# Four edits to the second stage's order of work: landmarks read from PSUM, a later bias product, another split of a norm, an earlier sum

## The chip, the cores and the metric

The kernel runs on one core of a Trainium2 chip, as one launch. Its time is the device time of that core in microseconds (us), the median of the runs shown. A core has five engines that run side by side: TensorE (PE, matrix products into PSUM), VectorE (DVE), ScalarE (ACT), GpSimd (POOL) and SyncE (SP, which here issues most transfers). They wait for each other only through semaphores.

## What is computed

Sixteen samples of 128 channels by 32 by 32 pixels pass through three layers. Only the third layer's first half and its gate matter here:

```python
# second stage, attention with landmarks (8 heads, 16 landmarks, N = 1024 tokens)
q_lm, k_lm = q[:, :, lm_idx], k[:, :, lm_idx]
kernel_1 = softmax(q @ k_lm.T * scale)      # keys' landmarks against all queries
kernel_2 = softmax(q_lm @ k_lm.T * scale)
kernel_3 = softmax(q_lm @ k.T * scale)
z = kernel_2.T / fro**2                     # then six Newton steps:
for _ in range(6):
    z = 2.0 * z - z @ kernel_2 @ z
out = kernel_1 @ (z @ (kernel_3 @ v))       # then the projection, and the sum with the input
# second stage, mixture of 8 experts, the best 2 for each token
gate = softmax(xt @ Wg); topv, topi = top_k(gate, 2); topv /= sum(topv) + 1e-6
h = gelu(xt @ W1[e] + b1[e]); ye = h @ W2[e] + b2[e]; out += ye * scores[:, e]
```

Before it stand an attention layer and a convolution layer, after it a dense attention with a mixture of 16 experts. The change leaves these as they are.

## The kernel before

The program runs in three stages: attention and convolution to about 2360 us, the landmark and GELU stage (`landmark_and_gelu_phase`, from L1058) to about 3900 us, and the dense stage. The change touches the middle one.

In it, every sample passes three jobs. `front` is the landmark attention. `choice` is the gate: a norm over each token, scores, the two best experts, the routing table, and the part of the result that comes from the experts' second bias. `experts` is the work of the 23 tiles of 128 routed rows. While `experts(i)` runs, `front(i + 2)` and `choice(i + 1)` run beside it; `front(0)` and `front(1)` with `choice(0)` run ahead of all expert work.

The order is written out by hand in slots. Each engine has a generator for each job; `yield 19` means that what follows belongs behind slot 19. `side_by_side` (L1186) goes through the 46 slots of a sample, two for each tile of rows; in each slot it issues the engine's own expert step and then, job by job in the order given (`front`, `choice`, `combine`), what has fallen due. So the slots fix the order on each engine, and semaphores hold one engine back for another. A late step holds up all that is behind it on its engine.

The parts that the change and the prediction name:

- Landmarks. TensorE forms queries and keys at slots 15 and 16 (L1679, L1681), both through L1662. ScalarE moves them from PSUM to `qt` and `kt` with their biases (L1576, L1579). VectorE picks every 64th column of both, spreads it over the heads with a block mask and writes `q_lm` and `k_lm` (L1354, slot 17). TensorE then forms the first score product (L1685, slot 18) and, from `kt`, the third (L1688, slot 19).
- Newton. TensorE multiplies (L1707), VectorE copies the product out of PSUM (L1406), TensorE multiplies twice (L1710, L1711), VectorE updates both forms of z (L1409, L1410). After the first update VectorE also sums the first softmax's weights (L1414) and inverts the sum (L1416); after the second it multiplies the weights by it (L1419).
- Norm of the gate's tokens, `token_norm_steps` (L976): statistics, variance, then an inverse root of ten small operations (L58 to L65), then the scaling (L991). In `choice`, statistics and variance are issued at slot 0 and the rest at slot 4 (L1500 to L1502). Also at slot 4, and ahead of it, `front` issues L1344 and L1346, on whose result TensorE's transposes (L1672, slot 6) wait. TensorE turns the scaled tokens with L1746 at slot 8.
- Bias product. TensorE multiplies scores by the second bias in two halves (L1776, slots 34 and 36), both into the PSUM tile `pc`; VectorE adds each half to the attention's result (L1526, slots 36 and 38). The second product waits for the first addition.
- Routing. VectorE writes the row numbers (L1473, slot 30), upon which POOL scatters the tokens with 16 indirect transfers (L1321). When all have landed, SP loads the next sample's first rows (L1246), which TensorE turns at slot 45 (L1784) and ScalarE moves out of PSUM (L1631). Behind that load SP issues the next weights of the experts (L1256).
- Expert tiles: TensorE L1801 (up), ScalarE L1617 (GELU), TensorE L1811 (down).

Of the kernel before, what the change touches and what calls it, by code (L numbers as in the profile page):

```python
# [21 lines left out]
AX = mybir.AxisListType  # L22
# [3 lines left out]
N = HW * HW  # L26
NT = N // 128
HALVES = N // 512
HEADS = 8
# [1028 lines left out]
def landmark_and_gelu_phase(nc, ctx, B, io, const, maps, gn2, x1_dram, x_dram, y_dram, score_dram, out):  # L1058
# [7 lines left out]
    with ExitStack() as st:  # L1066
# [6 lines left out]
        LM = 16  # L1073
        STEP = N // LM
# [28 lines left out]
        q_lm, k_lm = small[:, 7, :], small[:, 8, :]  # L1103
# [226 lines left out]
        def _(dve):  # L1330
            b16 = const["block16"].rearrange("p (h l) -> p h l", h=HEADS)

            def front(i):
# [17 lines left out]

                for src, dst, up in ((qt, q_lm, 1), (kt, k_lm, 2)):
                    dve.wait_ge(S["qk_up"], i * 2 + up)
                    last = dve.tensor_tensor(dst[:, :].rearrange("p (h l) -> p h l", h=HEADS), b16,  # L1354
                                             src[:, 0:N:STEP].unsqueeze(1).broadcast_to((128, HEADS, LM)), ALU.mult)
                last.then_inc(S["lm_up"], 1)
                yield 19
# [41 lines left out]

                dve.tensor_scalar(zt[:, :], m2[:, :], fro[:, :], None, ALU.mult).then_inc(S["z0_up"], 1)  # L1400

                for it in range(NEWTON):
# [9 lines left out]
                    if it == 0:  # L1412
                        dve.wait_ge(S["k1_exp"], i + 1)
                        dve.tensor_reduce(sum1[:, :], k1v, axis=AX.X, op=ALU.add)  # L1414
                        dve.drain()
                        dve.reciprocal(sum1[:, :], sum1[:, :])  # L1416
                        dve.drain()
# [77 lines left out]
            def choice(i):  # L1495
# [4 lines left out]
                for n, last in enumerate(token_norm_steps(dve, xln2, tok, stats2, mv2, var2, inv2, tmp2)):  # L1500
                    if n == 2:
                        yield 4  # L1502
# [20 lines left out]
                for k in range(HALVES):  # L1523
                    yield 36 + 2 * k
                    dve.wait_ge(S["b2_ps"], i * HALVES + k + 1)
# [40 lines left out]
        def _(act):  # L1566
            def front(i):
# [9 lines left out]
                yield 16  # L1577
                act.wait_ge(S["qk_ps"], i * 2 + 2)
                act.activation(kt[:, :], pa[:, :], ACT.Identity, bias=kb[:, :]).then_inc(S["qk_up"], 1)  # L1579
                yield 21  # L1580
# [76 lines left out]
        def _(pe):  # L1657
# [7 lines left out]
            def front(i):  # L1665
# [20 lines left out]
                last.then_inc(S["s1_ps"], 1)  # L1686
                yield 19
                wide(pa, q_lm[:, :], kt).then_inc(S["s3_ps"], 1)  # L1688
                yield 21
# [48 lines left out]
            def choice(i):  # L1738
# [29 lines left out]
                for k in range(HALVES):  # L1768
                    yield 34 + 2 * k
                    if k:  # L1770
# [546 lines left out]
```

## Time and profile before

| | |
|---|---|
| time, median of 3 runs | 5388.46 us (5380.94 to 5393.68) |
| the profiled execution | 5387.68 us, span 5385.9 us |
| busy: PE, DVE, ACT, POOL | 89%, 66%, 55%, 19% of the span |
| mean granted TensorE clock | 0.96 of full speed |
| middle stage, 2360 to 3900 us | PE 1343, DVE 911, ACT 826, POOL 499 us busy |

An engine's busy share is the time in which it works on instructions. In the rows further down, a number in brackets at the end is the time for which the engine stood idle before the instruction, and what it was released by. The time of the profiled execution holds 1.8 us beside its span.

### The profile page before, as it was taken

What the parts mean: (1) busy time and instruction counts of PE and PEld (TensorE: products, weight loads), DVE (VectorE), ACT (ScalarE), POOL (GpSimd) and SP (SyncE); (2) the same over time, 40 slices, a digit from 0 to 9 for tenths busy, and PEclk for the clock granted to TensorE, in tenths of its full rate; (3) what the DMA queues carried; (4) which work ended last, traced back from release to release, by engine and by line L of the source; (5) the groups of instructions that cost most, each with busy time, mean ns of one, the idle gap of its engine ahead of it and who ended that gap; (6) DMA issues with size and microseconds to landing.
All of it is one profiled execution on the core that took longest, in us unless ns stands there. A gap on an engine that the chain in (4) does not pass through costs nothing. (4 is left out here: it accounts for less than half of the span.)

```text
span 5385.9 us, 81280 instructions
## 1 busy us (share of the span) xinstructions
PE 4780.0 (89%) x25601; PEld 2597.7 (48%) x25601; DVE 3550.8 (66%) x7443; ACT 2946.7 (55%) x5390; POOL 1020.9 (19%) x1348
## 2 busy tenths in 40 slices
PE   5888888888888886977899999898999999999999
PEld 1222222222222221325888888888855555555554
DVE  6677777777777772555566666665577677776775
ACT  2665666666665654422555555555755555455552
POOL 2211211122121212211333343433210000000000
PEclk6999999999999998977999999999999999999999
DMA  2522222222222221232455555545321111111112
GB/s 83 152 72 72 72 95 72 72 72 72 72 76 81 72 76 32 29 71 76 146 171 147 170 160 160 173 139 151 115 60 50 49 56 46 53 50 49 56 46 77
DMA packets 406292, 477.05 MB, mean 89 GB/s; under 512 B 87640, under 2 KB 249648, under 8 KB 403760
## 3 DMA queue, kind: packets, MB, share of 16 engines
q1 hardware_dynamic: 372128, 424.84, 26.0%
q0 software_dynamic: 20576, 35.55, 2.4%
q10 hardware_dynamic: 13168, 11.48, 0.8%
q8 instruction: 213, 3.49, 0.3%
q14 instruction: 207, 1.70, 0.1%
HBM read 308.54 MB, written 145.57 MB: 84 GB/s over the span
## 5 line engine op out<-in xcount | busy, mean ns | idle before, releaser
L605 ACT ACTIVATE a_probs<-ps_b 128x512 f32<-128x512 f32 x2048 | 1111.1, 594 | 786.7 <-PE ps_b L701 773.9
L461 DVE TENSOR_REDUCE a_negmax<-ps_a 128x1 f32<-128x1024 f32 x1024 | 1206.2, 1220 | 382.1 <-PE ps_a L645 373.8
L645 PE MATMUL ps_a<-a_k_stack,a_q_stack 96*128 96x512 bf16 x2048 | 629.8, 393 | 177.2 <-DVE a_negmax L461 90.2
L701 PE MATMUL ps_b<-a_q_stack,a_k_stack 99*128 99x512 bf16 x2048 | 669.8, 389 | 65.8 <-ACT a_probs L605 30.9
L1617 ACT ACTIVATE n_hidden<-n_ps_h,n_b 128x128 f32<-128x128 f32 x1472 | 420.5, 373 | 413.3 <-PE n_ps_h L1801 409.8
L714 PE MATMUL ps_o<-a_probs,a_v_ones 128*32 128x512 f32 x4096 | 560.8, 620 | 0.2 <-ACT a_probs L605 0.2
L645 PEld LDWEIGHTS ps_a<-a_k_stack,a_q_stack 96*128 96x128 bf16 x2048 | 146.0, 98 | 726.9 <-DVE a_negmax L461 470.5
L1811 PE MATMUL n_ps_xy<-n_down_weights,n_hidden 128*128 x2944 | 405.3, 281 | 55.9 <-ACT n_hidden L1617 28.9
L701 PEld LDWEIGHTS ps_b<-a_q_stack,a_k_stack 99*128 99x128 bf16 x2048 | 195.1, 99 | 484.2 <-ACT a_probs L605 247.2
L1811 PEld LDWEIGHTS n_ps_xy<-n_down_weights,n_hidden 128*128 128x128 f32 x2944 | 366.0, 194 | 86.8 <-issue 83.0
L1801 PE MATMUL n_ps_h<-n_xy,n_up_weights 128*128 128x128 f32 x2944 | 402.9, 281 | 4.2 <-DMA n_up_weights<-in_L_ffn_W_dram 2.6
L2100 ACT ACTIVATE n_down_weights<-n_ps_h 128x512 f32<-128x512 f32 x288 | 172.5, 599 | 416.9 <-PE n_ps_h L2215 313.2
L1321 POOL DMA_INDIRECT rows_scratch<-n_xln,n_index_out x256 | 257.6, 1006 | 718.5 <-DVE n_index_out L1473 641.5
L1801 PEld LDWEIGHTS n_ps_h<-n_xy,n_up_weights 128*128 128x128 f32 x2944 | 372.8, 197 | 27.3 <-issue 23.8
L1313 POOL DMA_INDIRECT n_rows<-outs_scratch,n_index_back x256 | 261.7, 1022 | 363.8 <-DMA outs_scratch<-n_xy 246.9
L417 POOL CAST a_shift<-a_shift 16x128 bf16<-16x128 f32 x192 | 54.2, 283 | 1300.7 <-DVEq L470 1283.4
L2163 PEld LDWEIGHTS n_ps_f<-n_xln,n_u_probs_t 128*128 128x128 f32 x2048 | 246.2, 192 | 67.4 <-DVE n_u_probs_t L1982 36.4
L2163 PE MATMUL n_ps_f<-n_xln,n_u_probs_t 128*128 128x128 f32 x2048 | 250.9, 276 | 8.2 <-ACT n_u_probs_t L2066 8.2
L2156 PE MATMUL n_ps_f<-n_qt 128*128 128x512 f32 x512 | 240.9, 593 | 0.0
L2069 ACT ACTIVATE n_yt_probs<-n_ps_f,e_negmax 128x1024 f32<-128x1024 f32 x128 | 142.6, 1114 | 128.6 <-DVE e_negmax L1985 128.3
L1985 DVE TENSOR_REDUCE e_negmax<-n_ps_f 128x1 f32<-128x1024 f32 x128 | 156.5, 1222 | 77.0 <-PE n_ps_f L2156 76.3
L2203 PE MATMUL n_ps_c<-n_down_weights,n_xt 128*128 128x512 f32 x384 | 198.1, 599 | 2.6 <-DVE n_down_weights L2041 2.6
(345 smaller groups left out, 7398.5 us busy)
## 6 DMA issues: line engine op xcount, KB each, us to landing
n_up_weights<-in_L_ffn_W_dram SPq DMA_DIRECT2D x368, 256.0 KB
n_up_weights<-score_scratch SPq DMA_DIRECT2D x512, 128.0 KB, 2.9
split_scratch<-a_pieces SPq DMA_DIRECT2D x180, 256.0 KB
a_q_stack<-split_scratch SPq DMA_DIRECT2D x128, 192.0 KB, 3.4
a_k_stack<-split_scratch SPq DMA_DIRECT2D x128, 192.0 KB, 4.0
rows_scratch<-n_zero SPq DMA_DIRECT2D x16, 1472.0 KB
outs_scratch<-n_xy SPq DMA_DIRECT2D x176, 128.0 KB
n_xg<-rows_scratch SPq DMA_DIRECT2D x80, 256.0 KB, 3.8
```

What stands on the lines that cost most here:

```text
L461: dve.tensor_reduce(negmax[:, b, t:t + 1], bank, axis=AX.X, op=ALU.max, negate=True).then_inc(ring_read, 1)
L605: act.activation(probs[:, m % PROBS, 512 * k:512 * k + 512], ps_b[:, k, :], ACT.Exp).then_inc(b_exp, 1)
L645: last = pe.matmul(bank[:, cols], q_stack[0:KS, h, 128 * t:128 * t + 128], k_stack[0:KS, h, cols], start=True, stop=True)
L701: pe.matmul(ps_b[:, k, :], k_stack[:, h, 128 * t:128 * t + 128], q_stack[:, h, 512 * k:512 * k + 512], start=True, stop=True).then_inc(b_u ...
L714: last = pe.matmul(ps_o[32 * j:32 * j + 32, 512 * k:512 * k + 512], v_ones[:, t, J * g + j, :], probs[:, (J * quad + j) % PROBS, 512 * k:5 ...
L1313: gp.indirect_dma_start(rows[:, k, t, :], None, y_dram[i][:, :], bass.IndirectOffsetOnAxis(index_back[:, k, t:t + 1], 0)).then_inc(gathere ...
L1321: gp.indirect_dma_start(x_dram[i][:, :], bass.IndirectOffsetOnAxis(index_out[:, k, t:t + 1], 0), xln2[:, t, :], None).then_inc(scattered, 16)
L1617: last = act.activation(hidden[:, j % 2, f, :], ps_h[j % 2][:, 128 * f:128 * f + 128], ACT.Gelu, bias=b1[:, bass.ds(e, 1), f:f + 1].rearra ...
L1801: last = pe.matmul(ps_h[j % 2][:, 128 * f:128 * f + 128], up_weights[:, j % RING, 128 * f:128 * f + 128], rows_t, start=True, stop=True)
L1811: last = pe.matmul(ps_xy[:, col:col + 128], hidden[:, j % 2, f, :], own_down[:, f, :], start=(f == 0), stop=(f == FT - 1))
L2156: last = pe.matmul(pa[:, 512 * k:512 * k + 512], qt[:, 128 * t:128 * t + 128], qt[:, 512 * k:512 * k + 512], start=True, stop=True)
L2163: last = pe.matmul(pb[:, 0:C], probs_t[:, (t - 1) % 2, m, :], xln[:, m, :], start=(m == 0), stop=(m == NT - 1))
```

## The change

Four edits, all in `landmark_and_gelu_phase`:

1. `k_lm` is formed straight from the keys' product in PSUM, with the bias added in the same operation; VectorE waits for TensorE in place of ScalarE. ScalarE's pass over all keys now waits until the landmarks are formed. TensorE waits for `kt` ahead of the third score product.
2. The sum of the first softmax's weights is issued ahead of the first Newton step, behind the forming of z. Its inverse stays.
3. The inverse root of the gate's norm is issued at slot 0; only the scaling is left at slot 4.
4. The second half of the bias product goes from slot 36 to 39 on TensorE, and its addition from slot 38 to 40 on VectorE.

```diff
--- before.py
+++ after.py
@@ -1349,11 +1349,12 @@
                 token_norm(dve, xln, tok_next, stats, mv, var, inv, tmp).then_inc(S["ln_up"], 1)
                 yield 17
 
-                for src, dst, up in ((qt, q_lm, 1), (kt, k_lm, 2)):
-                    dve.wait_ge(S["qk_up"], i * 2 + up)
-                    last = dve.tensor_tensor(dst[:, :].rearrange("p (h l) -> p h l", h=HEADS), b16,
-                                             src[:, 0:N:STEP].unsqueeze(1).broadcast_to((128, HEADS, LM)), ALU.mult)
-                last.then_inc(S["lm_up"], 1)
+                every = lambda ap: ap[:, 0:N:STEP].unsqueeze(1).broadcast_to((128, HEADS, LM))
+                by_head = lambda ap: ap[:, :].rearrange("p (h l) -> p h l", h=HEADS)
+                dve.wait_ge(S["qk_up"], i * 2 + 1)
+                dve.tensor_tensor(by_head(q_lm), b16, every(qt), ALU.mult)
+                dve.wait_ge(S["qk_ps"], i * 2 + 2)
+                dve.scalar_tensor_tensor(by_head(k_lm), every(pa), kb[:, :], b16, ALU.add, ALU.mult).then_inc(S["lm_up"], 1)
                 yield 19
 
                 s1 = pb_[:, :].rearrange("p (g l) -> p g l", l=LM)
@@ -1398,6 +1399,9 @@
                 dve.tensor_scalar(z[:, :], m2t[:, :], fro[:, :], None, ALU.mult)
 
                 dve.tensor_scalar(zt[:, :], m2[:, :], fro[:, :], None, ALU.mult).then_inc(S["z0_up"], 1)
+                dve.wait_ge(S["k1_exp"], i + 1)
+                dve.tensor_reduce(sum1[:, :], k1v, axis=AX.X, op=ALU.add)
+                dve.drain()
 
                 for it in range(NEWTON):
                     yield NEWTON_AT + 2 * it
@@ -1410,9 +1414,6 @@
                     dve.scalar_tensor_tensor(zt[:, :], zt[:, :], 2.0, pa[:, 640:768], ALU.mult, ALU.subtract).then_inc(z_up, 1)
                     dve.drain()
                     if it == 0:
-                        dve.wait_ge(S["k1_exp"], i + 1)
-                        dve.tensor_reduce(sum1[:, :], k1v, axis=AX.X, op=ALU.add)
-                        dve.drain()
                         dve.reciprocal(sum1[:, :], sum1[:, :])
                         dve.drain()
                     if it == 1:
@@ -1498,7 +1499,7 @@
 
                     dve.wait_ge(scattered, i * 256)
                 for n, last in enumerate(token_norm_steps(dve, xln2, tok, stats2, mv2, var2, inv2, tmp2)):
-                    if n == 2:
+                    if n == 3:
                         yield 4
                 last.then_inc(S["ln2_up"], 1)
                 yield 12
@@ -1521,7 +1522,7 @@
                         yield 27 + n // 2
                 dve.drain().then_inc(S["owner_up"], 1)
                 for k in range(HALVES):
-                    yield 36 + 2 * k
+                    yield 36 + 4 * k
                     dve.wait_ge(S["b2_ps"], i * HALVES + k + 1)
                     dve.tensor_tensor(tokens[:, i, 4 * k:4 * k + 4, :].rearrange("p t c -> p (t c)"), tok[:, 4 * k:4 * k + 4, :].rearrange("p t c -> p (t c)"), pc[:, :], ALU.add).then_inc(S["base_up"], 1)
 
@@ -1576,6 +1577,7 @@
                 act.activation(qt[:, :], pb_[:, :], ACT.Identity, bias=qb[:, :]).then_inc(S["qk_up"], 1)
                 yield 16
                 act.wait_ge(S["qk_ps"], i * 2 + 2)
+                act.wait_ge(S["lm_up"], i + 1)
                 act.activation(kt[:, :], pa[:, :], ACT.Identity, bias=kb[:, :]).then_inc(S["qk_up"], 1)
                 yield 21
                 act.wait_ge(S["k1_sub"], i + 1)
@@ -1685,6 +1687,7 @@
                     last = pe.matmul(pb_[:, 128 * t:128 * t + 128], qt[:, 128 * t:128 * t + 128], k_lm[:, :], start=True, stop=True)
                 last.then_inc(S["s1_ps"], 1)
                 yield 19
+                pe.wait_ge(S["qk_up"], i * 2 + 2)
                 wide(pa, q_lm[:, :], kt).then_inc(S["s3_ps"], 1)
                 yield 21
                 pe.wait_ge(S["k1_sub"], i + 1)
@@ -1766,7 +1769,7 @@
                         last = pe.transpose(pc[0:E, 128 * t:128 * t + 128], gate["score"][:, 4 * k + t, :], ident)
                     last.then_inc(S["scores_ps"], 1)
                 for k in range(HALVES):
-                    yield 34 + 2 * k
+                    yield 34 + 5 * k
                     if k:
                         pe.wait_ge(S["base_up"], i * HALVES + 1)
                     else:
```

## Rows read from the trace of the kernel before

**Rows 1.** Waits, 2950 to 3640 us: us in total, times, longest.
```profile
PE n_ps_xy L1811 <- ACT n_hidden L1617: 16.4, 8, 2.3
DVE n_u_probs_t L1344 <- PE n_ps_f L1662: 15.7, 8, 5.8
...
PE n_ps_c L1776 <- DVE maps L1526: 10.9, 8, 1.4
...
PE n_ps_xy L1811 <- ACT n_xy L1631: 9.8, 9, 1.2
...
PE n_ps_c L1746 <- DVE n_xln L991: 8.0, 8, 1.2
PE n_ps_f L1710 <- DVE n_small L1406: 7.3, 16, 0.7
...
PE n_ps_f L1685 <- DVE n_small L1354: 5.8, 8, 0.9
```

**Rows 2.** Timeline, landmarks: start, us, engine, line, tiles, [idle before, releaser].
```profile
2398.80 1.38 PE L1685 MATMUL n_ps_f<-n_small,n_qt 128*128 128x128 f32 x10 [1.61 <-DVE n_small L1354]
...
3065.30 1.88 PE L1662 MATMUL n_ps_f<-n_xt,n_small 128*128 128x512 f32 x4
...
3068.28 1.13 ACT L1579 ACTIVATE n_kt<-n_ps_f,n_kb 128x1024 f32<-128x1024 f32 x1
...
3069.88 2.05 PE L1685 MATMUL n_ps_f<-n_small,n_qt 128*128 128x128 f32 x16 [0.69 <-DVE n_small L1354]
```

**Rows 3.** Timeline, the first Newton steps.
```profile
3000.26 0.29 DVE L1406 COPY n_small<-n_ps_f 128x128 f32<-128x128 f32 x1 [2.95 <-PE n_ps_f L1707]
...
3002.45 1.22 DVE L1414 TENSOR_REDUCE n_sum<-n_xln 128x64 f32<-128x1024 f32 x1
...
3004.42 0.29 DVE L1406 COPY n_small<-n_ps_f 128x128 f32<-128x128 f32 x1
...
3009.24 0.49 PE L1710 MATMUL n_ps_f<-n_small 128*128 128x128 f32 x2 [0.67 <-DVE n_small L1406]
```

**Rows 4.** Timeline, norm of the gate's tokens.
```profile
3044.99 1.28 DVE L1344 SCALAR_TENSOR_TENSOR n_u_probs_t<-n_ps_f,n_b,n_u_probs_t 128x1024 f32<-128x1024 f32 x1 [1.00 <-PE n_ps_f L1662]
...
3047.67 0.17 DVE L58 TENSOR_SCALAR n_gate_above<-n_gate_above 128x8 int32<-128x8 int32 x1
...
3048.58 1.04 PE L1672 MATMUL n_ps_f<-c_ident,n_u_probs_t 128*128 128x128 f32 x8
...
3050.11 2.21 DVE L991 TENSOR_SCALAR n_xln<-n_tok,n_gate_above 128x128 f32<-128x128 f32 x8
```

**Rows 5.** Timeline, from routing to the next sample's first rows.
```profile
3095.73 0.17 DVE L1473 CAST n_index_out<-n_place 128x16 uint32<-128x16 f32 x1
...
3116.23 1.01 POOL L1321 DMA_INDIRECT rows_scratch<-n_xln,n_index_out  x1 [0.31 <-issue]
...
3118.54 0.38 SPq L1246 DMA_DIRECT2D n_xg<-rows_scratch  x1
...
3121.41 0.44 PE L1784 MATMUL n_ps_xy<-c_ident,n_xg 128*128 128x128 f32 x2
```

**Rows 6.** DMA issues, 3118.3 to 3119.0 us: KB each, us to landing.
```profile
n_xg<-rows_scratch SPq DMA_DIRECT2D x1, 256.0 KB, 2.8
```

**Rows 7.** Timeline, the sample before: routing and first rows.
```profile
3010.86 0.17 DVE L1473 CAST n_index_out<-n_place 128x16 uint32<-128x16 f32 x1
...
3038.12 0.38 PE L1784 MATMUL n_ps_xy<-c_ident,n_xg 128*128 128x128 f32 x2
```

**Rows 8.** Timeline, clock: first rows, next routing, and L1722.
```profile
2774.57 0.44 PE L1784 MATMUL n_ps_xy<-c_ident,n_xg 128*128 128x128 f32 x2 [1.44 <-DMA n_xg<-rows_scratch]
...
2836.66 0.17 DVE L1473 CAST n_index_out<-n_place 128x16 uint32<-128x16 f32 x1
...
3024.75 3.50 PE L1722 MATMUL n_ps_f<-n_v,n_u_probs_t 128*128 128x128 f32 x16
```

**Rows 9.** Stretches: us, busy PE, PEld, DVE, ACT, POOL, clock, DMA, GB/s.
```profile
2776.00:2777.00 1.00, 0.92 (x4) 0.93 (x5) 1.00 (x6) 0.00 (x0) 0.00 (x0) 0.50 1.01 152
```

## The prediction, made before the changed kernel was run

> **What bounds the kernel now.** I read the busy shares first: TensorE is busy 89% of the span. So what can be won is what it stands idle for, and the change touches the second stage alone. There, sixteen samples follow each other; from one sample's routing to the next takes 84.87 us (3010.86 to 3095.73) [rows 5, 7]. The waits of eight such samples [rows 1] show why TensorE pauses: 0.73 us a sample for the key landmarks (5.8 by 8), 1.0 for the gate's normalized tokens, 0.91 for the two copies of the Newton product, 1.36 for the first half of the bias sum. That is 4.0 us a sample, 56 us over 14 samples, and would be the gain if TensorE alone set the pace.
>
> It does not. After routing (L1473), POOL issues 16 scatters, the last ending 21.5 us later; SP can only then load the first rows of the next sample, at 22.8; they take 2.8 us to land [rows 5, 6], and TensorE turns them (L1784) 25.68 us after routing. 3118.54 + 2.8 = 3121.34 against a start at 3121.41: they were awaited, though no pause is booked. So each sample has two parts: from the rows' arrival to routing, TensorE with its waits (57.6 us, 3038.12 to 3095.73 [rows 5, 7]), and from routing to the rows' arrival, a chain of POOL, SP and a transfer that nothing in the change shortens.
>
> **Landmarks.** Before, ScalarE adds the bias to all keys (1.13 us) and VectorE then picks the landmarks. Now VectorE reads PSUM, where the product ends at 3065.30 + 1.88 = 3067.18 [rows 2]. No row shows this operation; the bounds are 0.29 (a 128x128 copy from PSUM [rows 3]) and 1.28 (a 128x1024 operation with the same three operands [rows 4]), and I take 0.35, as it is 128x128. Landmarks stand at 3067.6; TensorE pauses 0.69 and starts at 3069.88, so could start at 3069.19. The whole pause goes: 0.72 a sample, 14 samples, 10 us. At 1.28 they would stand at 3068.5, still in time. The first two samples run without expert work beside them: of a pause of 1.61 [rows 2] the 0.35 and handovers remain, 1.15 twice, 2.3. The added wait holds ScalarE's bias pass, with a row move and the next hidden tile queued behind it; but that pass started at 3068.28, after hidden-tile work, 0.7 after the landmarks will be there. The third score product, which needs the keys, runs 2 us after the first. It costs nothing; were VectorE late, all of ScalarE would be. Sum 12.3 (bounds 8 to 13).
>
> **Sum of the key weights.** It moves from behind the first Newton step to ahead of it: 1.22 us [rows 3]. At its new place VectorE idles 2.95 us before the first copy, held by TensorE; 1.3 with the drain fits, so nothing is paid. At the old place it delays the second copy (3004.42). The pauses for two copies are 0.91 a sample, 0.67 of it the second [rows 3], which comes of a later multiply that stays but starts sooner. Bounds 0.24 (the first pause only) and 0.91 (both); I take the middle, 0.57: 8 us for 14. In the first two samples the sum lies on the path in either place: nothing.
>
> **Norm split.** The square root (ten small operations, 3050.11 − 3047.67 = 2.44 us [rows 4]) moves ahead of L1344. There VectorE waits 1.00 for TensorE in this sample, 1.96 on average [rows 1], so L1344 comes 1.44 later here. The transposes on its result started at 3048.58, about 0.95 after it was ready: TensorE loses 0.5. Against it, the scaling (L991) no longer follows the root and the pause of 1.0 goes: 0.5 net here, 1.0 where the wait is over 2.4. I take 0.75 for 14 samples and one more in the stage's tail: 11 us (bounds 0, if the delay eats it, and 15).
>
> **Bias product.** TensorE no longer pauses 1.36 for the half sum; the second half (its work stays) goes three slots later, behind the mixed product. VectorE's addition moves behind a 1.22 us addition that covers it; combine steps follow, and the copy for the next product (L1434) has over 1 us to spare. No moved step issues a transfer, and no queue of SP or POOL is passed. But all this lies between routing and the first rows, so it pays only where TensorE comes to them late. It does where the clock had fallen: of the 14, four come 1.0 to 1.3 after the landing, such as 27.26 [rows 7], the others within 0.2. That is 5 us, not 19 (bounds 0 and 19).
>
> **The clock.** L1722 took 3.50 us for 16 products at the lower level (1.2 GHz), half the full one [rows 8]; such falls follow the 1.36 pause in 8 of 14 samples and should go, but their cost is mostly inside the cover just named. New is a longer pause ahead of the next sample: TensorE now arrives 1.36 sooner than 25.68, at about 24.3, and waits till the rows land at 25.6, 1.3 us, then another 1.1 for the move (9.8 by 9 [rows 1]). Where that sum was 1.3 or less the clock never fell (11 samples); where it was 1.65 or more, it did, thrice, such as after 1.44 + 1.07 [rows 8]: granted 0.50 [rows 9]. After the pause of 2.1 for the hidden tile [rows 1] it falls in 6 of 13. So I expect 8 falls in 14, five more than now. One costs 1.2 to 2.5 us: the samples that have it took 60.9 to 62.1 from the rows to routing, those with only the other fall 59.6. Minus 8, with 0 and −16 as ends.
>
> **Sum.** 12.3 + 8 + 11 + 5 − 8 = 28.3. The profiled execution took 5387.68 us (span 5385.9 and 1.8 around it), 0.8 below the median of 5388.46: 5387.7 − 28.3 = 5359.4, so 5360 for the median.
>
> **Rivals.**
> - *No new falls.* The pause ahead of the next sample grows and the clock holds, as it did in 7 of 13 pauses of 2.1 us. Then the last term is zero: 5387.7 − 36.3 = 5351. Against: all three longer pauses at this very place had a fall. 0.18. The Trainium skill ("TensorE: Matmul & The Clock Gate", section "Why this matters for your kernels") warns only of idle gaps longer than any this change makes, and would make this rival certain; the granted clock [rows 8, 9] already disagrees with it.
> - *The clock takes it all (slower).* Place: the first rows of each sample. The slowest sample took 62.1 from these rows to routing (2774.57 to 2836.66 [rows 8]), against a mean of 59.0 over 13 samples. If all 14 did, +43, less the 31 of the first three terms, and none of the fourth: 5400. It decides from 2.2 us a sample upwards. For it: all three longer pauses had a fall. Against: only one row is that bad, and it holds two falls. 0.06.
> - *The pauses all count.* If the rows did not bind (SP or the landing gets quicker as traffic shifts), TensorE's 1.36 and the 8 falls of 1.6 (half of 3.50 is 1.75, a little of it covered) would come back too: 31 of the first three terms, 19 and 13 off, 5325. Against: [rows 5, 6] leave 0.07 us. 0.07.
> - *VectorE's order eats it (no change).* The split costs L1344 and everything after it more than 0.95 of slack, ScalarE waits for a late landmark; only the sum's 8 us are kept and 0.2 a sample is lost to the split: 5387.7 − 8 + 14 × 0.2 = 5382. For it: VectorE is in order and the root stands in front. 0.07.
>
> **Numbers.** 0.62 for the forecast, which with the rival without falls makes 0.80. The ends of the terms do not all fall together: at the low end 12.3, 12, 15, 5 and no falls (44 off) give 5343, at the high end 10, 3, 5, 5 and −16 (7 off) give 5381; the range is 5342 to 5381. About 0.2%, 11 us, is what a measurement of this kernel can tell from no change. Faster than 5377.7: 0.80; within: 0.13; slower than 5399.2: 0.07.
>
> **What would show it.** TensorE's waits for L1354, L991 and L1526 gone; those for L1406 down to a third; the time from arrival to routing 1.9 shorter in samples with like clock; L1473 to L1784 at 25.6 in nearly all, with a wait for the rows of about 1.3; L1722 at 1.95 everywhere; falls of the clock now after L1784. Wrong if L1473 to L1784 sinks below 25, if ScalarE waits for the landmarks, or if L1672 waits for VectorE by more than 0.7.

## The result, and the profile after

The changed kernel takes 5354.61 us (median of 4 executions, 5346.64 to 5359.09) against 5389.16 for the kernel before (4 executions). The ratio is 0.9936 with a 95% interval of 0.9918 to 0.9954. The forecast was 5360, with a range of 5342 to 5381. The profiled execution took 5346.64 us (span 5344.8), 41.0 less than the one profiled before. All line numbers behind L1354 are one to three higher now. Of all executions below, one of `e6_half_scatter` ran at a mean granted clock of 0.74 and took 6173.8 us; it is left out of that kernel's median.

**Where the 41 us are.** Sixteen routings divide the second stage. The first stands at 2492.09 us (before 2492.47), the last at 3749.27 (before 3787.01), and 1595.6 us follow it (before 1598.9). So 37.4 us lie between the first routing and the last, 3.3 behind it, and 0.4 ahead of it. I then took the samples one by one from the timeline. The middle thirteen take 83.66 us each on average, before 85.98. From routing to the next sample's first rows it is 26.10 (before 26.95), and from there to the next routing 57.56 (before 59.03).

The first view is TensorE's waits of the kernel after, in the same stretch as [rows 1], 2950 to 3640 us (us in total, times, longest):

```profile
PE n_ps_xy L1814 <- ACT n_hidden L1619: 16.4, 8, 2.2
PE n_ps_xy L1787 <- DMA n_xg<-rows_scratch: 13.1, 8, 3.7
PE n_ps_xy L1814 <- ACT n_xy L1633: 8.6, 8, 1.1
PE n_ps_f L1713 <- DVE n_small L1410: 5.4, 8, 0.7
PE n_ps_c L1749 <- ACT n_xt L1600: 3.6, 9, 0.4
```

The waits for the landmarks, for L991 and for the half sum (5.8, 8.0 and 10.9 in [rows 1]) are gone. The copies' wait fell from 16 times to 8. Two waits are new: L1787 waits for the rows in every sample, 1.6 us on average here, where before only a few samples did, and L1749 waits 0.4 for ScalarE where it had waited 1.0 for VectorE.

The timeline of the kernel after, one sample from routing to the first rows, answers to [rows 5] (start, us, engine, line, tiles, [idle before, releaser]):

```profile
3075.93 0.17 DVE L1474 CAST n_index_out<-n_place 128x16 uint32<-128x16 f32 x1
...
3098.49 0.38 SPq L1246 DMA_DIRECT2D n_xg<-rows_scratch  x1
...
3101.29 0.44 PE L1787 MATMUL n_ps_xy<-c_ident,n_xg 128*128 128x128 f32 x2 [1.06 <-DMA n_xg<-rows_scratch]
...
3102.80 1.15 PE L1814 MATMUL n_ps_xy<-n_down_weights,n_hidden 128*128 x8 [1.07 <-ACT n_xy L1633]
```

The step is 25.36 us, as it was in the sample of [rows 5] (25.68), but now with a wait of 1.06 booked in front of it, and behind it the 1.07 for the move. Seven of the 14 samples are like it (25.4 to 25.6 us, wait 1.0 to 1.25). In the other seven the load is issued or lands later, the step is 26.0 to 28.2 and the wait 1.6 to 3.8. What follows is seen in one-microsecond slices (us, busy PE, PEld, DVE, ACT, POOL, clock, DMA share, GB/s):

```profile
3103.00:3104.00 1.00, 1.00 (x9) 0.84 (x8) 1.00 (x5) 0.00 (x0) 0.00 (x0) 0.92 0.75 187
3104.00:3105.00 1.00, 1.00 (x5) 1.00 (x6) 0.95 (x5) 0.00 (x0) 0.00 (x0) 0.50 1.00 267
3105.00:3106.00 1.00, 1.00 (x6) 1.00 (x6) 0.82 (x10) 0.00 (x0) 0.00 (x0) 0.50 0.95 325
```

TensorE is busy throughout, but at the lower level, 1.2 GHz. Most such falls last 3.4 us. One stands behind the first rows in 12 of 14 samples (before in 3), and there are 19 falls in all between the first sample's first rows and the last's (before 18). These two counts are of one execution. The same kernel was profiled a second time (`a1_after_again`, below): again 19 falls, but eight behind the first rows and eleven behind the pause of 2.1 us for a hidden tile (L1814, the first wait of the list), against 12 and seven here. So where the clock falls differs between executions of one and the same program. In that second execution a sample with nearly the same two pauses reads:

```profile
3101.93 0.44 PE L1787 MATMUL n_ps_xy<-c_ident,n_xg 128*128 128x128 f32 x2 [1.09 <-DMA n_xg<-rows_scratch]
3103.45 1.15 PE L1814 MATMUL n_ps_xy<-n_down_weights,n_hidden 128*128 x8 [1.07 <-ACT n_xy L1633]
```

```profile
3105.00:3106.00 1.00, 1.00 (x11) 0.96 (x10) 0.93 (x8) 0.07 (x1) 0.00 (x0) 1.00 1.08 347
```

The granted clock stays at 1.00 there.

The timeline of the landmarks, the answer to [rows 2]:

```profile
3131.16 0.35 DVE L1357 SCALAR_TENSOR_TENSOR n_small<-n_ps_f,n_kb,c_block 128x128 f32<-128x128 f32 x1 [0.66 <-PE n_ps_f L1664]
...
3132.21 1.13 ACT L1581 ACTIVATE n_kt<-n_ps_f,n_kb 128x1024 f32<-128x1024 f32 x1
...
3132.96 1.95 PE L1687 MATMUL n_ps_f<-n_small,n_qt 128*128 128x128 f32 x16
```

The operation that no row had shown takes 0.35 us, L1687 waits for nothing, and ScalarE's pass over the keys starts as soon as its hidden tile is done. Only in the first two samples, which have no expert work beside them, does ScalarE wait for the landmarks (2.28 us where it had waited 1.77 for TensorE). Two more timelines of the kernel after, L1725 as the answer to the last row of [rows 8] and the norm as the answer to [rows 4]:

```profile
3087.04 1.95 PE L1725 MATMUL n_ps_f<-n_v,n_u_probs_t 128*128 128x128 f32 x16
...
3110.89 1.23 DVE L1346 TENSOR_TENSOR n_u_probs_t<-n_u_probs_t 128x1024 f32<-128x1024 f32 x1
3112.03 2.31 DVE L991 TENSOR_SCALAR n_xln<-n_tok,n_gate_above 128x128 f32<-128x128 f32 x8
...
3117.89 0.66 PE L1749 MATMUL n_ps_c<-c_ident,n_xln 128*128 128x128 f32 x4 [0.40 <-ACT n_xt L1600]
```

The scaling (L991) now follows the sum L1346 at once. L1725 stands at 1.95 in all samples but the first (2.01); before, nine of sixteen took 3.4 to 3.8, such as the 3.50 in [rows 8].

### The profile page after: what moved, and what is told of

Read it like the earlier page. It is cut to its first block and busy times, and to the rows that moved or that the text cites. A ratio compares the mean times of both kernels' runs of the same rounds, so it can differ in the third digit from the quotient of the medians.

```text
span 5344.8 us, 81296 instructions
## 1 busy us (share of the span) xinstructions
PE 4765.3 (89%) x25601; PEld 2591.8 (48%) x25601; DVE 3551.8 (66%) x7443; ACT 2943.8 (55%) x5390; POOL 1012.0 (19%) x1348
## 5 line engine op out<-in xcount | busy, mean ns | idle before, releaser
L1814 PE MATMUL n_ps_xy<-n_down_weights,n_hidden 128*128 x2944 | 400.8, 280 | 55.8 <-ACT n_hidden L1619 28.8
L1804 PE MATMUL n_ps_h<-n_xy,n_up_weights 128*128 128x128 f32 x2944 | 415.8, 287 | 1.6 <-issue 1.3
L1814 PEld LDWEIGHTS n_ps_xy<-n_down_weights,n_hidden 128*128 128x128 f32 x2944 | 363.8, 193 | 84.6 <-issue 82.8
L1804 PEld LDWEIGHTS n_ps_h<-n_xy,n_up_weights 128*128 128x128 f32 x2944 | 383.7, 202 | 25.1 <-issue 21.7
```

The source lines that it names most:

```text
L1804: last = pe.matmul(ps_h[j % 2][:, 128 * f:128 * f + 128], up_weights[:, j % RING, 128 * f:128 * f + 128], rows_t, start=True, stop=True)
L1814: last = pe.matmul(ps_xy[:, col:col + 128], hidden[:, j % 2, f, :], own_down[:, f, :], start=(f == 0), stop=(f == FT - 1))
```

## The experiments

Twelve kernels ran: each part of the change alone, the change without one part, and edits at the first rows. The first four ran on one chip, the next four on a second and the last four on a third. Each group has its own runs of the kernel before beside it (5380.29, 5389.79 and 5383.55 us), so runs of different groups are compared by their ratios.

### Each part alone

`e1_landmarks` is the kernel before with the landmark edit alone:

```diff
-                    dve.wait_ge(S["qk_up"], i * 2 + up)
-                    last = dve.tensor_tensor(dst..., b16, src[:, 0:N:STEP]..., ALU.mult)
+                dve.tensor_tensor(by_head(q_lm), b16, every(qt), ALU.mult)
+                dve.wait_ge(S["qk_ps"], i * 2 + 2)
+                dve.scalar_tensor_tensor(by_head(k_lm), every(pa), kb[:, :], b16, ALU.add, ALU.mult)
...
+                act.wait_ge(S["lm_up"], i + 1)
...
+                pe.wait_ge(S["qk_up"], i * 2 + 2)
```

> The kernel before with the landmark edit alone. Theory A (what lies ahead of routing counts whole, what lies behind it is hidden by POOL's scatters and the load of the first rows): the stretch from the first rows (L1784) to routing (L1473) falls by 0.7 us against 57.6 to 57.9 in samples without a fall of the clock, the stretch from routing to the first rows stays at 25.6 to 27.3; about 11 us in all, 5378. Theory B (VectorE's order eats it, ScalarE waits for the landmark): the first stretch stays, 5388.

`e2_sum` is the kernel before with the sum of the key weights alone:

```diff
+                dve.wait_ge(S["k1_exp"], i + 1)
+                dve.tensor_reduce(sum1[:, :], k1v, axis=AX.X, op=ALU.add)
+                dve.drain()
                 for it in range(NEWTON):
...
                     if it == 0:
-                        dve.wait_ge(S["k1_exp"], i + 1)
-                        dve.tensor_reduce(sum1[:, :], k1v, axis=AX.X, op=ALU.add)
-                        dve.drain()
```

> The kernel before with the earlier sum of the key weights alone. Theory A: first rows to routing 0.57 us shorter in samples without a fall of the clock, 8 us in all, 5381; the pauses of TensorE for the copy of the Newton product fall from 0.91 to about 0.35 us a sample. Theory B (the sum only moves the delay to the first copy): nothing, 5389.

`e3_norm` is the kernel before with the norm split alone:

```diff
-                    if n == 2:
+                    if n == 3:
                         yield 4
```

> The kernel before with the norm split alone. Theory A: the wait of TensorE for L991 (1.0 us a sample) goes, half a us comes back at the transposes L1672 or at the copy that frees the PSUM tile; first rows to routing 0.5 to 0.75 us shorter, 7 to 11 us in all, 5380. Theory B (L1344 comes late and takes all back): nothing or up to 3 us slower.

`e4_bias` is the kernel before with the bias product alone:

```diff
-                    yield 36 + 2 * k
+                    yield 36 + 4 * k
...
-                    yield 34 + 2 * k
+                    yield 34 + 5 * k
```

> The kernel before with the later bias product alone. Theory A (the first rows bind): TensorE's pause of 1.36 us goes, but a wait of 1 to 1.3 us for the first rows takes its place; routing to first rows falls only from a mean of 26.95 to about 26.1, first rows to routing grows by about 1 us where the clock now falls behind the longer pause; in all between 5 us faster and 5 us slower. Theory B (TensorE's pauses all count): routing to first rows falls to 24.3, and 19 us or more are won, 5369 or less.

Measured, 10 executions of each: landmarks 5371.21 us, ratio 0.9988 (0.9979 to 0.9998); sum 5374.06, 0.9987 (0.9976 to 0.9998); norm split 5384.23, 1.0009 (0.9999 to 1.0019); bias product 5382.47, 1.0000 (0.999 to 1.0011). By ratio the first two gain 6.5 and 7.0 us, where 11 and 8 were expected; the third shows its theory B, the fourth its theory A.

What the traces add is finer than these. Between first rows and routing, a sample in which the clock did not fall in that stretch took 57.7 us before (7 samples, 57.3 to 57.9). It takes 56.5 to 57.1 with the landmarks (0.85 less on average), 56.7 to 57.5 with the sum (0.7 less), and 57.4 to 58.0 with the norm split: nothing. TensorE's waits in the kernel with the sum show that the first copy's wait went and the second one's, 0.7 a sample, stayed:

```profile
PE n_ps_f L1710 <- DVE n_small L1409: 5.4, 8, 0.7
```

In this stretch the copies' waits fell by 1.9 us (7.3 to 5.4) and a small one of L1707 for the update of z by 1.0 (1.2 to 0.2): 0.36 a sample. The other half of the 0.7 shows in no wait.

In the timeline of the kernel with the norm split, one sees why it gained nothing:

```profile
3122.83 1.09 PE L1672 MATMUL n_ps_f<-c_ident,n_u_probs_t 128*128 128x128 f32 x8 [0.56 <-DVE n_u_probs_t L1346]
...
3127.66 0.66 PE L1746 MATMUL n_ps_c<-c_ident,n_xln 128*128 128x128 f32 x4 [0.40 <-ACT n_xt L1598]
```

Of the pause of 1.0 for L991, 0.4 comes back as a wait for ScalarE's copy, and 0.56 as a wait for the delayed L1346. (In the eight samples 3.2 and 2.4 of the 8.0 us come back so; the rest shows in no wait, but the samples are no shorter.) In the kernel with the bias product alone TensorE's waits read:

```profile
PE n_ps_xy L1784 <- DMA n_xg<-rows_scratch: 12.7, 8, 3.7
```

The 10.9 us for L1526 are gone, and 12.7 for the rows stand there instead, 1.36 and 1.59 a sample. In this kernel the clock falls behind the first rows in all 14 samples. Those with this one fall of 3.4 us and no other take 58.6 to 59.0 us to the next routing, 1.15 more than the 57.7 without one. From routing to the rows the mean sank by 0.98 (26.95 to 25.97), from the rows to the next routing it rose by 0.85 (59.03 to 59.88). So this edit alone sells a pause ahead of the rows and buys a fall of the clock behind them.

### The change without one part, and idle products

Since the four ratios multiply to 0.9984 only, the change itself ran again (`a1_after_again`, no edit), beside two kernels that lack one part each and one with an addition.

> The changed kernel once more, beside runs of the kernel before on the same chip. The four edits alone gave ratios of 0.9988, 0.9987, 1.0009 and 1.0000, a product of 0.9984, against 0.9936 for all four in the first measurement. Theory A (the first measurement had few runs, but the stretches of the profile add up: 0.85 and 0.7 us a sample ahead of routing, 0.4 for the norm split once the clock falls at the first rows, 0.85 behind routing): 0.994 to 0.996. Theory B (the edits do add like their ratios): 0.998.

`e5_no_bias` puts the bias product back (the diff of `e4_bias`, reversed, on the kernel after):

> The changed kernel with the bias product put back to slots 36 and 38. Theory A (the later product wins 0.85 us a sample behind routing and loses 1.15 ahead of it by the fall of the clock at the first rows, of which the norm split regains 0.4): first rows to routing about 56.1 without a fall against 56.9, routing to first rows 26.9 against 26.1; in all within 4 us of the changed kernel. Theory B (the bias product is what makes the other three pay): 10 to 20 us slower than the changed kernel.

`e10_no_norm` puts the norm back (the diff of `e3_norm`, reversed, on the kernel after):

> The changed kernel with the norm split put back. Theory A (with the clock fallen at the first rows VectorE waits 1.2 to 3.5 us for TensorE ahead of L1344, which hides the root, so the split that was worth nothing alone is worth 0.4 us a sample here): 6 us slower than the changed kernel; TensorE waits 1.0 us a sample for L991 again. Theory B (the split is a loss in either company, 5 us alone): 5 us faster than the changed kernel.

`e8_fill` adds two products that nobody reads, ahead of the transposes of the next sample's first rows:

```diff
                         elif not isinstance(i, int) or i + 1 < B:
+                            if i + 2 < B:
+                                for _ in range(2):
+                                    pe.matmul(pa[:, 0:384], wproj[:, :], wqkv[:, :], start=True, stop=True)
                             turn_rows(i + 1, 0)
```

> The changed kernel with two idle products (128x384, results unused, into PSUM that is free there) on TensorE ahead of the turn of the next sample's first rows, where it waits 1.0 to 1.3 us. It leaves nothing out. Theory A (the pause of that wait and of the move together makes the clock fall, 1.15 us a sample in 13 of 13): the falls behind the first rows go in the samples with a wait near 1.1, first rows to routing falls from 56.9 to about 56.1, 8 to 12 us faster than the changed kernel. Theory B (the pause of 1.1 for the move is enough by itself, or the products delay the rows): as the changed kernel, or 3 us slower.

Measured: the change again 5350.48 us, ratio 0.9926 (0.9913 to 0.994); without the bias product 5353.23, 0.9936 (0.9923 to 0.995); without the norm split 5358.02, 0.9942 (0.9928 to 0.9955); with the idle products 5344.64, 0.9913 (0.9898 to 0.9928).

The change again lies below the 0.994 to 0.996 of its theory A, and far from theory B. Without the bias edit the time is the same within the intervals. Its trace has 10 falls against 19. Samples without one take 55.8 to 56.4 from rows to routing, 1.7 less than before, about the 0.85 and 0.7 of the two parts alone. Without the norm split 7.5 us are lost; the intervals overlap, but each of its executions (5354.83 to 5367.78) is slower than each of the change (5346.04 to 5353.07). Samples with one fall behind the rows and one behind the hidden tile take 58.1 to 58.4 from rows to routing in the kernel after, and 58.6 to 59.1 without the split: here it is worth 0.6 a sample. Alone it was worth nothing, and in the kernel without the bias edit 0.1 (1.7 less the 0.85 and 0.7, by subtraction; no kernel has the landmarks and the sum alone). VectorE's waits for L1344 tell why. The first fence is the kernel with the split alone, the second the one without it, the third the kernel after:

```profile
DVE n_u_probs_t L1344 <- PE n_ps_f L1662: 4.5, 2, 3.7
```

```profile
DVE n_u_probs_t L1344 <- PE n_ps_f L1664: 34.3, 9, 6.9
```

```profile
DVE n_u_probs_t L1344 <- PE n_ps_f L1664: 12.0, 8, 3.5
```

Without the split VectorE idles 3.8 us a sample ahead of L1344 beside the bias edit, and 1.96 in the kernel before [rows 1]. The root, 2.44 [rows 4], fits the first gap and not the second. The gap is that wide because TensorE, held up by its wait for the rows and then by a fall, comes late with the product that L1344 reads. Counted from the first rows, L1344 starts at 6.6 to 7.7 us in the kernel before, in samples with at most 0.2 us of wait and no fall there, and the split alone puts it at 8.2 to 8.8. With wait and fall it stands at 8.0 to 8.3 in most samples without the split, and at 8.0 to 8.4 with it. The half scatters (below) test this: that kernel has the bias edit and the split but no wait for the rows, and there VectorE never waits for TensorE ahead of L1344, and TensorE waits 4.3 us for L1346 in eight samples. So the split pays where TensorE has waited for the rows, which the bias edit brings about; the bias edit without that wait is not enough.

It also has a price, in the second sample, which has no expert work beside it. There the transposes of L1674 wait in the kernel after (first) and in the kernel without the split (second):

```profile
2445.69 1.97 PE L1674 MATMUL n_ps_f<-c_ident,n_u_probs_t 128*128 128x128 f32 x8 [5.37 <-DVE n_u_probs_t L1346]
```

```profile
2447.18 1.97 PE L1674 MATMUL n_ps_f<-c_ident,n_u_probs_t 128*128 128x128 f32 x8 [2.95 <-DVE n_u_probs_t L1346]
```

The 2.4 us between the two waits are near the root that now stands ahead of L1344. In the second execution of the kernel after the same wait is 4.71.

The idle products take about 6 us off. The timeline of that kernel shows them (L1838) in the place of the wait:

```profile
3099.84 1.46 PE L1838 MATMUL n_ps_f<-n_small 128*128 128x384 f32 x4
3101.45 0.44 PE L1787 MATMUL n_ps_xy<-c_ident,n_xg 128*128 128x128 f32 x2 [0.15 <-DMA n_xg<-rows_scratch]
```

That is less than the 8 to 12 of theory A, and the intervals overlap (executions 5339.36 to 5346.74 against 5346.04 to 5353.07). The rows' step comes no sooner (26.12 against 26.10), but the falls behind it sink from 12 or eight to four. These four are in the samples in which a wait for the rows of 0.57 us or more is left (up to 2.5); in the other ten it is at most 0.42. The three samples without any fall take 55.2 to 56.1. Ten of the 14 falls are now behind the pause for the hidden tile, the one of 2.1 us. So the fall behind the first rows belongs to the wait ahead of them: fill it, and it goes; it does not come back in full at the next pause (14 falls against 19).

### Is it the chain behind the routing?

`e6_half_scatter` leaves out half of the scattered rows (the second choice of each token), so that POOL's part of the chain is half as long:

```diff
-                    for k in range(K):
+                    for k in range(1):
...
-                    sp.wait_ge(scattered, 256 * (i + 1))
+                    sp.wait_ge(scattered, 128 * (i + 1))
```

> The kernel after, with only the first choice of each token written to its slot: 8 of 16 scatters a sample, so half of the scattered rows are left out, and the waits behind them count 128 instead of 256. Theory of the prediction (the first rows hang on the chain routing, POOL's scatters, SP's load, its landing, and TensorE waits for that): from routing to the first rows' step falls from 25.4 to about 24.3 us with no wait for the load, nearly no clock fall behind it is left, and the time is 5315 to 5330 us. Rival (TensorE's own order sets the step, and the load lands beside it): no change beyond 3 us, and the step stays at 25.4 us.

`e7_half_scatter_no_bias` leaves out the same and puts the bias product back:

> The same kernel with half of the scatters left out, and the bias product and its addition put back where they stood before. Theory (the later product gains a pause of about 1.3 us ahead of the first rows, as soon as the rows are there in time): about 1.3 us a sample dearer than the run with half of the scatters alone, 14 samples, so some 15 to 20 us slower than it. Rival (the later product gains nothing in itself): within 4 us of it.

Measured: 5324.41 us (three executions), ratio 0.9887 (0.9867 to 0.9907), and with the bias product back 5336.68, 0.9912 (0.9895 to 0.9928). The first lies in the range of the theory, some 21 to 26 us below the kernel after by ratio (0.9926 and 0.9936), which excludes the rival that TensorE's own order sets the step in the kernel after; L1787 no longer waits for the rows in the list of TensorE's waits:

```profile
PE n_ps_xy L1814 <- ACT n_hidden L1619: 18.4, 9, 2.2
PE n_ps_xy L1814 <- ACT n_xy L1633: 8.7, 8, 1.2
PE n_ps_f L1713 <- DVE n_small L1410: 6.0, 9, 0.7
PE n_ps_f L1674 <- DVE n_u_probs_t L1346: 4.3, 8, 0.7
PE n_ps_c L1749 <- ACT n_xt L1600: 3.2, 8, 0.4
```

The step came out as expected: 24.14 to 24.30 us in the middle samples, with no wait ahead of it. The load is issued nine us sooner than in the kernel after (13.42 against 22.56), and TensorE turns the rows when its own order comes to them:

```profile
3062.93 0.17 DVE L1474 CAST n_index_out<-n_place 128x16 uint32<-128x16 f32 x1
...
3080.90 0.27 PE L1787 MATMUL n_ps_xy<-c_ident,n_xg 128*128 128x128 f32 x1
...
3087.07 0.38 PE L1787 MATMUL n_ps_xy<-c_ident,n_xg 128*128 128x128 f32 x2
```

(The single transpose at 17.97 us behind routing is that of the last, odd tile of the running sample, on the same line, and stands at 17.97 in the kernel after as well. The next sample's first rows are the pair behind it.) No fall follows the first rows in any of the 14 samples, where "nearly none" was expected. But each of the 13 middle samples has one behind the hidden tile's pause. The timeline of the first kernel and a slice of its clock:

```profile
3131.89 1.89 PE L1814 MATMUL n_ps_xy<-n_down_weights,n_hidden 128*128 x8 [2.11 <-ACT n_hidden L1619]
```

```profile
3133.00:3134.00 1.00, 1.00 (x7) 1.00 (x6) 0.00 (x0) 0.00 (x0) 0.00 (x0) 0.50 0.00 0
```

With the bias product back the step is 25.56 to 25.65 us in ten of the 13 samples:

```profile
3068.20 0.18 DVE L1474 CAST n_index_out<-n_place 128x16 uint32<-128x16 f32 x1
...
3093.76 0.38 PE L1787 MATMUL n_ps_xy<-c_ident,n_xg 128*128 128x128 f32 x2
```

So the edit gains its full 1.4 us there, as TensorE's pause of 1.36 goes and no wait for the rows takes its place. In time it is worth 12.3 us, a little less than the 15 to 20 expected, and with the chain as it is 0 to 3. The falls decide how much of the gain stays. In eight of the 13 samples the kernel with the bias product back has no fall, and its period from routing to routing, 81.6 to 82.0 us, is as short as that of the other kernel with its fall behind the hidden tile (81.8 to 82.2): there the 1.4 are paid back in full. The gain comes from the other five, 83.3 to 85.1 us, which hold its six falls. No run shows whether another execution has its falls in the same places.

### A shorter way to the rows

`e9_early_rows` leaves nothing out. It issues the first steps of the routing sooner on VectorE:

```diff
-                        yield 27 + n // 2
+                        yield 27 + (n // 4 if n < 8 else n // 2)
```

> The kernel after, with the first four pairs of the routing's steps issued two turns sooner on VectorE, nothing left out. Theory (the chain from the routing bounds the first rows): the routing ends some 1 to 1.5 us sooner against TensorE's order, the wait for the load of about 1.1 us goes, and the time falls by 8 to 15 us below the kernel after. Rival (VectorE has no room for it: what stands behind the earlier steps comes later by as much): within 3 us of the kernel after, with new waits of TensorE for VectorE.

`e11_early_fill` has this and the idle products:

> The earlier routing steps and the two idle products ahead of the first rows' transposes together, nothing left out. If the idle products gain by keeping the granted clock up across a wait, and the earlier routing takes that wait away, the two hardly add: about the better of the two alone, some 5335 to 5342 us. Rival (each gains in its own place): the sum of both, below 5335 us. If the earlier routing gains nothing: as the idle products alone, 5343 to 5347 us.

Measured: 5335.66 us, ratio 0.9914 (0.9897 to 0.993), and 5338.41, 0.9919 (0.9902 to 0.9935). By ratio the first is 6 to 12 us below the kernel after (0.9926 and 0.9936), the lowest of the kernels that leave nothing out in us, though level by ratio with the one with the idle products (0.9913). The two do not add. TensorE's waits with the earlier routing:

```profile
PE n_ps_xy L1814 <- ACT n_hidden L1619: 18.3, 9, 2.1
PE n_ps_f L1713 <- DVE n_small L1410: 10.8, 8, 1.6
PE n_ps_xy L1814 <- ACT n_xy L1633: 8.6, 8, 1.1
PE n_ps_f L1710 <- DVE n_small L1414: 6.7, 9, 1.0
PE n_ps_f L1674 <- DVE n_u_probs_t L1346: 4.6, 6, 1.1
PE n_ps_c L1749 <- ACT n_xt L1600: 3.2, 8, 0.4
PE n_ps_xy L1787 <- DMA n_xg<-rows_scratch: 2.3, 2, 1.9
```

Both theories were half right. The wait for the rows fell from 13.1 to 2.3 us, 1.35 a sample. But the Newton products wait for VectorE 12 us more (10.8 and 6.7 against 5.4 and 0.2), 1.5 a sample. The sum of all pauses in the stretch is larger, 57.0 us against 49.7. What is smaller is the number of falls of the clock, 4 instead of 19, and with it the period of a sample: 82.43 us on average against 83.66 and 83.49 in the two executions of the kernel after, 1.1 to 1.2 less, 14 to 16 us for thirteen. That the falls are what makes it shorter is argued from these counts; no kernel changes the falls alone.

## Why the forecast held, and where it did not

**Landmarks (12.3).** Right in mechanism, a little short a sample: 0.85 instead of 0.72. In the first two samples the pause fell from 1.61 to 0.45, the 1.15 as forecast. How much of these 2.3 us remains there is not settled. The time from these samples' first transposes (L1672) to the first routing is 115.47 us before, 114.45 and 112.41 in the two executions of the kernel after, and 112.19 without the norm split. The split's wait in the second sample, 5.37 and 4.71 where it was 2.68, takes a part back, a cost that the forecast had not looked for in those samples.

**Sum of the key weights (8).** Right in size, 0.7 a sample against 0.57, and only in part in its working. The copies' wait was to fall to a third and fell by a quarter (7.3 to 5.4 us in eight samples), which is the low bound of 0.24 a sample. A wait of L1707 that the sum did not count gave 0.13 more, and the rest shows in no wait. That the size fits is partly luck.

**Norm split (11).** The term that was mis-sized. Alone it measured nothing or a small loss (1.0009), in the change 0.6 a sample by the traces and 7.5 us by its return. The step that failed is "the scaling no longer follows the root and the pause of 1.0 goes". It went, but 0.4 of it became a wait for ScalarE's copy L1600, a chain that the forecast did not follow; and the slack ahead of L1344, which the forecast took from the kernel before, is set by another part of the same change: by TensorE's wait for the rows and the fall behind it, which come with the bias edit.

**Bias product (5) and clock (−8).** Right in mechanism and nearly in their sum. The rows did bind: 25.36 us and a wait of 1.06 where 25.6 and 1.3 were forecast, in half of the samples, with longer ones in the others. TensorE's own arrival, forecast at about 24.3, is 24.14 in the kernel that does not wait for them (`e6_half_scatter`). The gain behind the routing was 0.98 alone. Falls behind the first rows came in 12 samples of 14 in one execution, in the forecast's eight in the other, and in all 14 with the bias product alone, so that the eight is not a count that this kernel keeps. Their price was 1.15 each, just under the 1.2 to 2.5. (That range rests on 59.6 us for samples with only the other fall; these three took 59.45, 60.00 and 60.04, on average 59.8, which makes it 1.0 to 2.3.) By the single edits, 14 × 0.98 is 13.7 gained and 14 × 0.85 is 11.9 paid: 2 us, against −3 by the forecast. Both terms are larger than the 5 and 8 forecast and cancel, so that the fit of their sum is in part luck. The 5 counted only samples in which TensorE came late; but the step also shrank in samples that the landing had bound, such as the sixth and the ninth (28.02 and 27.58 us before, 26.06 and 26.41 with the bias product alone). The ratio of this part alone, 1.0000, agrees. The rival without new falls is excluded by the granted clock. The rival in which the clock takes it all had the right place and too high a price: it took 2.2 a sample, the traces show 1.15. The rival in which the pauses all count did not come about, and the half scatters show the condition under which the 1.36 of the bias product does: they took 5324.41. That this is near the rival's 5325 is chance, since a fall stands in every middle sample there, where the rival had them go.

The Trainium skill, "TensorE: Matmul & The Clock Gate", section "Why this matters for your kernels", warns of idle gaps longer than the 1.06, 1.07 and 2.11 us of these pauses. The traces disagree with it once more: the granted clock fell to 0.50 behind a wait of 1.06 and one of 1.07, and behind one of 2.11. Two waits for the rows, 3.76 and 3.71 us, are longer than the forecast had this change make; a fall follows them too.

**The total.** The forecast was 28.3 us, the medians give 34.6, the two profiles 41.0. The parts by the traces are 14 × 0.85 + 14 × 0.7 + 14 × 0.6 + 2 = 32 us, between the forecast and the medians.

**The signs.** The waits for L1354, L991 and L1526 are gone, L1722 stands at 1.95, and the step never sinks below 25, as said. Two signs of being right failed: the copies' wait, and the time from rows to routing in samples with like clock. The only like pair (a fall behind the rows and one behind the hidden tile) is 60.86 us before against 58.1 to 58.4, 2.6 shorter rather than 1.9. Two signs of being wrong did show, in the first two samples alone: ScalarE waits for the landmarks, and L1672 waits 5.37 us for VectorE.

**What stays open.** The single edits, by their ratios, give 0.0016 together, 8.6 us, the whole change 34.6 to 39.3. The profiled executions seem to add up: against the profiled one of before (5387.68) the four stand at 5371.18, 5377.24, 5383.14 and 5378.90, together 40.3 us lower, the change 41.0. This shows nothing, since one execution of before stands in that sum four times and in the change once: with the median of before on the chip of the four, 5380.29, in its place, the sum is 10.7. The kernel before took 5380.29 us as a median on the chip of the four and 5389.79 on the chip of the change again, and the change did not run on the former.

The kernels that lack one part narrow it down. The norm split accounts for some 13 us of the gap of 31 (0.9984 against 0.9926): 7.5 us gained beside the others and 5 lost alone. The three edits without it measured 0.9942 on one chip, while their single ratios multiply to 0.9975, 18 us less. So most of the gap has nothing to do with the split. Whether it is the chip, or that the landmarks and the sum gain more together than apart, stays open; a kernel with these two alone, beside the four on one chip, would tell.

## What to carry to other kernels

A pause that is moved from one place to another is not neutral: the clock can fall behind it, so count the falls, not only the waits, and in more than one execution. In a kernel whose stage has two parts, one bound by an engine and one by a chain, a repair in the second part is worth its full pause only after the chain is shorter; here the same edit was worth 0 to 3 us, then 12.3, and what was left of it hung on where the clock fell. Where several edits touch one engine's order, take the slack of each from the order with the others in it.

## What was not expected of the hardware

The same pause has different results, even in one program: 12 falls behind the first rows in one execution of the kernel after, eight in the other. The wait of 2.1 us for the hidden tile stands in every kernel. Behind it the clock fell in 13 of 13 middle samples with half of the scatters, and in 2 of 13 with the earlier routing. There the timeline and the slice behind such a wait read:

```profile
3136.93 1.15 PE L1814 MATMUL n_ps_xy<-n_down_weights,n_hidden 128*128 x8 [2.11 <-ACT n_hidden L1619]
```

```profile
3137.00:3138.00 1.00, 1.00 (x9) 1.00 (x10) 0.59 (x3) 0.60 (x3) 0.00 (x0) 1.00 0.00 0
3138.00:3139.00 1.00, 1.00 (x11) 1.00 (x10) 0.29 (x1) 0.60 (x1) 0.00 (x0) 1.00 0.00 0
```

The clock is 1.00 where it was 0.50 in the other kernel. So the length of a pause alone does not decide; what else does, none of the runs settles. And three kernels with 10, 14 and 19 falls in their profiled executions (5343.6, 5342.6 and 5344.8 us of span) hardly differ in time. The first keeps the pause of 1.36 us a sample for the half sum, the second pays 1.46 of idle products; that this is why is not shown.
